# Where the second LayerNorm is done: per batch in attention, or per group after the rows are read back

## The reference

```python
x = x + tanh(g_xattn[0]) * attn(layernorm(x), ctx, ctx, gamma)    # 16 batches, 8 heads, [16, 128, 512] f32
x = x + tanh(g_ffn[0])   * ffn(layernorm(x), ...)                 # 2048 rows of 512
def layernorm(x):                                                 # no scale, no bias
    return (x - mean(x, -1)) / sqrt(var(x, -1) + 1e-5)
def ffn(x):                       # top-2 of 8 experts, hidden 256 to 1024
    h = x @ down_w + down_b
    topv, topi = top_k(softmax(x @ router_w + router_b - 1e-7 * cost), 2)
    gate = softmax(topv)
    out = sum over k, e of gate_k * (topi_k == e) * (gelu(gelu(h) @ w1_e + b1_e) @ w2_e + b2_e)
    out = (out + 0.1 * shared(h)) @ up_w + up_b
    return out + gelu(x) @ core_w + core_b
```

## Time and profile before

| | us |
|---|---|
| median of 3 runs (lowest, highest) | 695.79 (694.21, 697.62) |
| the profiled execution's own time | 693.51 |
| its span, first to last instruction | 690.6 |
| PE busy in the span | 651.6 (94%) |
| DVE | 515.6 (75%) |
| ACT | 531.1 (77%) |
| POOL | 468.1 (68%) |

### The profile page before, as it was taken

One profiled execution on the slowest core, in us unless ns is written; L12 is line 12 of the kernel. 1 busy time (PEld: TensorE's weight loads), 2 busy tenths in 40 slices (PEclk: granted clock), 3 DMA queues, 4 the chain that ended last, 5 costly groups with the idle time before them and its releaser, 6 DMA issues.

```text
span 690.6 us, 18438 instructions
## 1 busy us (share of the span) xinstructions
PE 651.6 (94%) x6005; PEld 342.6 (50%) x6005; DVE 515.6 (75%) x859; ACT 531.1 (77%) x1125; POOL 468.1 (68%) x468
## 2 busy tenths in 40 slices
PE   1799999999999999999999999989999999999998
PEld 0122222222222222222345655579999998998744
DVE  3989999999999999999789877853444434444466
ACT  2389999999999999999888568567777776776411
POOL 3688898888888879986737443506756656665722
PEclk9999999999999999999999999999999999999999
DMA  6755776666767666656335653579988998696596
GB/s 195 249 168 195 221 242 199 194 187 189 221 197 228 198 180 202 190 173 210 113 123 170 228 190 123 171 166 173 125 146 116 127 130 109 99 122 91 61 299 252
DMA packets 128482, 120.40 MB, mean 174 GB/s; under 512 B 64132, under 2 KB 97668, under 8 KB 128392
## 3 DMA queue, kind: packets, MB, share of 16 engines
q1 hardware_dynamic: 114968, 104.09, 53.5%
q0 software_dynamic: 12192, 14.16, 13.7%
q10 hardware_dynamic: 1232, 0.98, 0.5%
HBM read 60.25 MB, written 49.10 MB: 158 GB/s over the span
## 4 chain that ended last, share of the span: by engine, by line
PE 65%; DMA 13%; POOL 11%; DVE 4%; ACT 3%; issue 2%; SPq 2%; POOLq 0%; DVEq 0%
PE EH L1333 23%; PE Y L1333 15%; PE pv L571 11%; PE ring L558 7%; PE nat L546 4%; DMA QS<-q_scratch 2%; DMA q_scratch<-qhl 2%; ACT P L642 2%; POOL wlo L812 1%; DMA u<-in_wall 1%; DMA rd<-den_scratch 1%; DMA QS<-mrow 1%; DMA k_scratch<-khl 1%; POOL y_sums L2235 1%; DMA x_rows<-ao 1%
## 5 line engine op out<-in xcount | busy, mean ns | idle before, releaser
L717 DVE TENSOR_REDUCE mx<-nat 128x2 f32<-128x1024 f32 x256 | 296.6, 1212 | 14.1 <-PE nat L546 13.8
L642 ACT ACTIVATE P<-ring 128x512 f32<-128x512 f32 x512 | 281.1, 601 | 16.8 <-PE ring L558 10.9
L2235 POOL DMA_INDIRECT y_sums<-ysb,to x74 | 124.8, 1687 | 81.6 <-DVE ysb L2165 62.5
L571 PE MATMUL pv<-P,VT 128*32 128x256 f32 x2048 | 157.6, 391 | 0.4
L546 PE MATMUL nat<-KS,QS 48*128 48x512 f16 x512 | 113.1, 394 | 20.2 <-DMA QS<-q_scratch 14.0
L558 PE MATMUL ring<-QS,KS 49*128 49x512 f16 x512 | 119.3, 391 | 9.1 <-ACT P L642 6.8
L1333 PE MATMUL EH<-XA,whi 128*128 128x256 f16 (+1 forms) x688 | 104.9, 258 | 0.5 <-DMA XA<-g_rows 0.5
L1333 PE MATMUL Y<-whi,u 128*128 x592 | 104.3, 273 | 0.2
L571 PEld LDWEIGHTS pv<-P,VT 128*32 128x32 f32 x2048 | 43.9, 108 | 99.1 <-issue 49.1
L2115 DVE TENSOR_TENSOR u<-X,u 128x512 f16<-128x512 f32 x62 | 42.7, 689 | 62.1 <-ACT u L1739 59.0
L558 PEld LDWEIGHTS ring<-QS,KS 49*128 49x128 f16 x512 | 30.7, 93 | 111.1 <-ACT P L642 88.5
(11 more groups left out here) (282 smaller groups left out, 1039.2 us busy)
## 6 DMA issues: line engine op xcount, KB each, us to landing
QS<-q_scratch SPq DMA_DIRECT2D x64, 96.0 KB, 2.7
KS<-k_scratch SPq DMA_DIRECT2D x62, 96.0 KB, 2.3
u<-in_wall SPq DMA_DIRECT2D x7, 640.0 KB, 4.0
X<-in_x SPq DMA_DIRECT2D x16, 256.0 KB, 3.3
q_scratch<-qhl SPq DMA_DIRECT2D x16, 256.0 KB, 2.2
xr<-in_x SPq DMA_DIRECT2D x16, 256.0 KB, 3.5
rd<-den_scratch SPq DMA_DIRECT2D x16, 256.0 KB
u_rows<-un SPq DMA_DIRECT2D x16, 256.0 KB
```

The lines of the kernel that those rows point to most:

```text
L571: m = pe.matmul(pv[32 * j:32 * j + 32, q], VT[i][:, lb, g, j, :], Pb[4 * (s % 2) + j][:, q], start=(lb == 0 and half == 0), stop=(lb == 3) ...
L642: act.activation(Pb[4 * (s % 2) + j][:, :], bank[:, :], ACT.Exp).then_inc(t_use.sem, 1)
L717: dve.tensor_reduce(mx[:, k // 8, :, k % 8], nat[k % 2][:, :, :], AX.X, ALU.max).then_inc(t_max.sem, 1)
L2235: pool.indirect_dma_start(out=ysum[:, :], out_offset=bass.IndirectOffsetOnAxis(ap=to[:, j % 2, a:a + 1], axis=0), in_=ysb[j % 2][:, a, :], ...
```

## The change

Batches 0 to 3 (group 0) are left as they were. For batches 4 to 15 attention does no second LayerNorm: `xstats`, `xaggr`, `xnegm`, `xveps`, `xrstd` and `u` go; SP stores the raw rows `ao` to u_rows as soon as `x1` is done, and `x1t` writes to `un`, which goes to x_rows. So `nb` of a later batch waits for the store to u_rows, where it waited for that to x_rows. Each of the groups 1 to 3 is normalised in its buffer: `row_stats(r)` on DVE, then `normed(r)` on POOL, for which PE's `uT` waits.

```diff
 dve_small(w):
-               ([(w - 3, "xstats"), (w - 3, "xaggr")] if w >= 3 else []) + \
+               ([(w - 3, "xstats"), (w - 3, "xaggr")] if 3 <= w < 3 + G4 else []) + \
 pool_jobs(w):
         if w >= 3:
-            jobs += [(w - 3, n) for n in ("xnegm", "xveps", "xrstd", "u", "x1t")]
+            if w < 3 + G4:
+                jobs += [(w - 3, n) for n in ("xnegm", "xveps", "xrstd", "u")]
+            jobs.append((w - 3, "x1t"))
 sync, window w, s = w - 3:
-                ck.wait(t_pool, s, "u")
-                sp.dma_start(us[s], un[:, :]).then_inc(t_us.sem, 16)
+                ck.wait(t_pool, s, "u" if s < G4 else "x1")
+                sp.dma_start(us[s], un[:, :] if s < G4 else ao[s % 2][:, :]).then_inc(t_us.sem, 16)
 tensor, uT:
-                if i == 0:
-                    wait(pe, t_uu[r % 2], r)
                 for t in range(G4):
+                    if i == 0 and r == 0:
+                        wait(pe, t_uu[0], r)
+                    elif i == 0:
+                        wait(pe, t_nu, r, t)
+        def row_stats(r):
+            wait(dve, t_uu[r % 2], r)
+            for t in range(G4):
+                if r > 1:
+                    wait(dve, t_mv, r - 1, t)
+                dve.bn_stats(sx[:, t, :], ub[r][:, t, :]).then_inc(t_sx.sem, 1)
+            for t in range(G4):
+                wait(dve, t_sx, r, t)
+                if t == 0 and r > 1:
+                    wait(dve, t_ln, r - 1, "veps")
+                dve.bn_aggr(mv[:, t, :], sx[:, t, :]).then_inc(t_mv.sem, 1)
 low_0:
+            row_stats(1)
 rest, after each of DVE's operations o:
-                    if o == (1, "r", "ms"):
-                        ends["late"]["vector"]()
+                    if o == (1, "gl", 1):
+                        row_stats(2)
+                    elif o == (0, "core", G4 - 1):
+                        row_stats(3)
+        def normed(r):
+            wait(pool, t_mv, r, G4 - 1)
+            if r > 1:
+                wait(pool, t_nu, r - 1, G4 - 1)
+            pool.tensor_scalar(ln[:, :, 0], mv[:, :, 0], -1.0, None, ALU.mult).then_inc(t_ln.sem, 1)
+            pool.tensor_scalar(ln[:, :, 1], mv[:, :, 1], EPS, None, ALU.add).then_inc(t_ln.sem, 1)
+            wait(pool, t_ln, r, "veps")
+            pool.tensor_tensor(ln[:, :, 2], ln[:, :, 1], cst[:, K_PH:K_PH + 1].broadcast_to([P, G4]), ALU.pow).then_inc(t_ln.sem, 1)
+            wait(pool, t_ln, r, "rstd")
+            for t in range(G4):
+                pool.tensor_scalar(ub[r][:, t, :], ub[r][:, t, :], ln[:, t, 0:1], ln[:, t, 2:3], ALU.add, ALU.mult).then_inc(t_nu.sem, 1)
 rest, POOL:
+            normed(1)
             for r in BODIES:
                 for o in seq("pool", r):
...
                     elif o == (0, "sc", G4 - 1):
                         last_norm()
+                        normed(2)
+                    elif o == (1, "sc", G4 - 1):
+                        normed(3)
```

More of the change, by code:

```diff
@@ L196, in program @@
             "rbb": sb("rbb", [P, G4, E]), "tb": sb("tb", [P, L]), "lp": sb("lp", [P, L]),
+            "mv": sb("mv", [P, G4, 2]), "ln": sb("ln", [P, G4, 3]),
             "gb": sb("gb", [P, NT]), "zs": sb("zs", [P, LAT]), "Z": sb("Z", [P, LAT]),
@@ L491, in body @@
             if s >= 0:
-                ck.wait(t_pool, s, "u")
-                sp.dma_start(us[s], un[:, :]).then_inc(t_us.sem, 16)
+                ck.wait(t_pool, s, "u" if s < G4 else "x1")
+                sp.dma_start(us[s], un[:, :] if s < G4 else ao[s % 2][:, :]).then_inc(t_us.sem, 16)
                 ck.wait(t_pool, s, "x1t")
-                sp.dma_start(x1s[s], ao[s % 2][:, :]).then_inc(t_st.sem, 16)
+                sp.dma_start(x1s[s], ao[s % 2][:, :] if s < G4 else un[:, :]).then_inc(t_st.sem, 16)
                 tail.get((w, "loads"), lambda: None)()
@@ L515, in last_x1 @@
             sp.wait_ge(t_pool.sem, t_pool.at[B - 1, "x1t"])
-            sp.dma_start(x1s[B - 1], ao[(B - 1) % 2][:, :]).then_inc(t_st.sem, 16)
+            sp.dma_start(x1s[B - 1], un[:, :]).then_inc(t_st.sem, 16)
         def last_u():
-            sp.wait_ge(t_pool.sem, t_pool.at[B - 1, "u"])
-            sp.dma_start(us[B - 1], un[:, :]).then_inc(t_us.sem, 16)
+            sp.wait_ge(t_pool.sem, t_pool.at[B - 1, "x1"])
+            sp.dma_start(us[B - 1], ao[(B - 1) % 2][:, :]).then_inc(t_us.sem, 16)
         late["sync"] = last_x1, last_u
@@ L722, in body @@
                 small(ck, *job)
[L724 to L728, removed]
         over_windows(dve, body, tail)
@@ L741, in job @@
             elif what == "nb":
-                ck.wait(t_st, b - 2)
+                ck.wait(t_st if b - 2 < G4 else t_us, b - 2)
                 done(pool.tensor_scalar(ao[i][:, :], U[1][:, :], cme[:, 1:2], 1.0, ALU.mult, ALU.mult))
@@ L767, in job @@
             elif what == "x1t":
-                ck.wait(t_pool, b, "u")
-                done(pool.tensor_tensor(ao[i][:, :], ao[i][:, :], keep["tb"][:, :], ALU.add))
+                ck.wait(t_pool, b, "u" if b < G4 else "x1")
+                if b == G4:
+                    ck.wait(t_us, b - 1)
+                elif b > G4:
+                    ck.wait(t_st, b - 1)
+                done(pool.tensor_tensor((ao[i] if b < G4 else un)[:, :], ao[i][:, :], keep["tb"][:, :], ALU.add))
             elif what == "negm":
@@ L832, in last_norm @@
         def last_norm():
-            for what in ("xnegm", "xveps", "xrstd", "u", "x1t"):
-                job(Clock(pool), B - 1, what)
+            job(Clock(pool), B - 1, "x1t")
         def last_rows():
@@ L913, in ffn @@
     uf = A("uf", [P, LB, L])
+    mv, ln = keep["mv"], keep["ln"]
     gbs = u[:, :, :].rearrange("p t q -> p (t q)").bitcast(F16)
@@ L933, in ffn @@
     ro, wo, bo, eo = (A(n, [P, NJ], I32) for n in ("ro", "wo", "bo", "eo"))
+    sx = ro[:, 0:6 * G4].bitcast(F32).rearrange("p (t c) -> p t c", t=G4)
     bcur = A("bcur", [P, 2, 8])
@@ L998, in ffn @@
     scattered = lambda r, i: t_sf[i - 2] if r == 0 and i >= 2 else t_sc[i]
+    t_sx, t_mv, t_ln, t_nu = T("f_row_stats"), T("f_row_mean"), T("f_row_scale"), T("f_normed")
     t_zr = T("zero_rows", 16)
@@ L1068, in ffn @@
                 tally.plan(*o)
+    for r in range(1, NG):
+        for t in range(G4):
+            for t_ in (t_sx, t_mv, t_nu):
+                t_.plan(r, t)
+        for what in ("negm", "veps", "rstd"):
+            t_ln.plan(r, what)
     for r in range(NG):
@@ L2075, in set_up, with low_0 @@
             do(0, "lpc", 0)
-        def select_0():
+        def low_0():
             for o in ops_0[LB + 1:upto((0, "r", "dz"))]:
                 do(*o)
-        def low_0():
             dve.wait_ge(t_in2.sem, t_in2.value)
+            row_stats(1)
             for o in ops_0[upto((0, "r", "dz")):upto((0, "gl", 1))]:
@@ L2166, in collect @@
                               ALU.mult).then_inc(t_dve.sem, 1)
-        return {(B - 2, "recip"): set_up, (B - 2, "xstats"): select_0, (B - 1, "recip"): low_0}, rest
+        return {(B - 2, "recip"): set_up, (B - 1, "recip"): low_0}, rest
     def gpsimd(pool):
@@ L2242, in rest @@
                 pool.tensor_tensor(*summands(n), ALU.add).then_inc(t_pool.sem, 1)
-        return {(2, "whi"): output_bias, (B - 3, "xnegm"): some(("uhp", 0), ("uhp", 1)),
+        return {(2, "whi"): output_bias, (B - 3, "x1t"): some(("uhp", 0), ("uhp", 1)),
                 (B - 2, "att"): some(("uhp", 2), ("uhp", 3))}, rest
```

## The result

The changed kernel took 700.36 us (median, 699.37 to 703.54) against 695.60 us of the kernel before in the same comparison: a ratio of 1.0080, 95% interval 1.0064 to 1.0097, 4.8 us between the medians. The prediction was 699.3 (695.0 to 702.7), with 0.48 on no change and 0.45 on slower by over 0.5%. It is slower by 0.8%, with the whole interval above 0.5%: the outcome that had 0.45, not the one that had 0.48. The time came out near the forecast, but partly from other places: two of its terms after attention were far off, in opposite directions.

A forecast was written before the change was run, and what follows sets the result against it. The prediction took PE and ACT, not DVE, to set the pace of attention. Its terms, -0.5 + 0.2 + 1.6 + 2.2 = +3.5 us, on 695.79 gave 699.3 us, with a range of all from 695 to 702.7.

The forecast's parts named there:

- The pace of attention: Attention windows: PE and ACT make the period, DVE follows with some 0.24 us to spare; removing its work gains 0.
- The first rival: Attention: DVE was the pace after all, giving -2.6 us in total, 693.2 us; chance 0.12.
- POOL and the store, -0.5: Attention: nb waits for the earlier u_rows store, so late queries land sooner; -0.5 us (0 to -1).
- Statistics of group 1, +0.2: DVE ahead of gl of group 0: the second gl comes late for PE's rt; +0.2 us (0 to 1).
- Normalising group 1 hidden: POOL after attention: 4.3 us of work ends before ACT copies uT's first tile; 0 (up to 1.5).
- PE found waiting for `uT`: After attention: a sign that would make the prediction wrong; no idle of PE before uT of group 1 was expected.
- Statistics of group 2, +1.6: DVE between second gl and Gp of group 1: PE's gt waits; +1.6 us (0.9 to 2.3).
- Statistics of group 3 hidden, up to 0.5: DVE ahead of gul and ul of group 2: PE reads ul late enough to hide 2.75 us; up to 0.5.
- Normalising group 3, +2.2: POOL ahead of gl of group 2: gl follows 4.3 us later and PE's rt waits; +2.2 us (1.6 to 2.9).
- more waits than counted: Rival, after attention: POOL held up by DVE in all three normed, larger stalls; +6.9 us, 702.7 us; chance 0.2.

The follow-up runs named there:

- e6: Kernel before, with the statistics of windows 7 to 15 taken over 8 of 512 columns, so less DVE time; 695.07 us, 1.0006.
- e9: Changed kernel in which POOL's nb also waits for the x_rows store of two batches before; 701.19 us, 1.0105.
- e5: e1 with row_stats(3) moved on DVE behind ul(1) of group 2; 695.04 us, 1.0018 of the kernel before.
- e10: e5 with row_stats(1) behind gl(1) of group 0 instead of ahead of both gl; 704.13 us, 1.0159 of the kernel before.
- e1: Changed kernel with normed(3) moved behind POOL's first gl of group 2; 696.28 us, 1.0032 of the kernel before.
- e2: Changed kernel with row_stats(3) one operation earlier on DVE, ahead of the last core of group 0; 700.70 us, 1.0090.
- e3: e2 with normed(3) also moved on POOL ahead of group 1's last scatter; 697.27 us, 1.0041 of the kernel before.
- e8: Kernel before with two more bn_stats per window on DVE in windows 7 to 15; 702.93 us, 1.0142.
- e11: Kernel before, unchanged, run again as a control; 695.11 us, 1.0010.
- e12: Changed kernel, unchanged, run again; 701.62 us, 1.0115 of the kernel before.
- e4: e3 with row_stats(1) also moved ahead of DVE's wait for the tables; 697.17 us, 1.0041 of the kernel before.

## Why the prediction was right or wrong

*The pace of attention: right, and shown.* DVE follows with 0.17 us to spare per window (I read 0.24 from the idle). The change took 0.68 us a window from it for nothing. The first rival, DVE as the pace, falls with e6. That the period is made by PE and ACT instead is still argued from the waits of the earlier trace rows: no run changed their work.

*POOL and the store, -0.5: wrong, shown by e9.* I tied the windows that ran over 19.95 us to queries that are late because of `nb`. From window 8 on the longest window is 20.22 us before and 20.04 in the changed kernel's two profiles, but the stretch up to the `uf` copy is no shorter there. It was a guess, and took the only gain of the sum.

*Statistics of group 1, +0.2: mis-sized.* 0.65 us at `rt`, of which 0.18 is given back before `rk` of group 1; 0.47 stays (+0.49 in e5). My time for the second `gl` was good: 364.05 forecast, 363.29 + 0.68 = 363.97 measured. That is partly luck: the statistics began 0.52 us later than I had them (358.46), behind a wait that I had not counted, and a `gat` instruction between the two `gl` that took 1.25 us before took 0.16. And PE came there 0.39 us sooner than before, and I had summed the two as if they were independent: what PE gains ahead of a wait for DVE, the wait takes back.

*Normalising group 1 hidden: right in cost, not to the letter.* PE found waiting for `uT` was to be a sign that the prediction is wrong, and `uT` does wait 0.42 us for its tiles. But the wait for ACT behind it shrinks from 1.55 to 0.71 us, and `a` is then as far behind (+0.28) as `rt` was (+0.26): it costs nothing. e10 shows what it costs 3 us later.

*Statistics of group 2, +1.6: wrong in size, 0.23.* The largest error among the terms that I had worked out. DVE was not 0.4 us later against PE at this place, as I had assumed from group 1, but 0.1 (`msum` 0.18 us later, `rk` 0.08). And the `pk` operations went from 1.35 to 0.29 us and `carry` from 0.50 to 0.17, 1.39 us of holds gone where I counted 0.5. POOL before, then DVE and POOL after:

```profile
383.27 1.26 POOL L769 TENSOR_TENSOR ao<-ao,tb 128x512 f32<-128x512 f32 x1
```

```profile
381.64 2.46 DVE L2072 BATCH_NORM_STATS2 ro<-u 128x6 f32<-128x512 f32 x4
...
384.81 0.29 DVE L1860 TENSOR_TENSOR pk<-rk,m 128x32 f32<-128x32 f32 x2
...
383.17 1.28 POOL L771 TENSOR_TENSOR un<-ao,tb 128x512 f32<-128x512 f32 x1
```

POOL's `x1t`, which had stood beside `pk` (383.34 in the earlier trace rows), now falls on `bn_stats`, and that is not slowed (2.46 us for four here and 2.46 in front of `gul`, where POOL only issues scatters). By the forecast's own sum, with these: 2.75 - 0.25 - 0.8 + 0.1 - 1.39 = 0.41. The Trainium skill's SBUF — State Buffer, section Who interferes with whom, puts the conflict on DVE operations with two SBUF inputs or in a two-port mode; `bn_stats` with one input left alone agrees. I had used that rule for the upper end only, and not asked which DVE instruction would meet POOL's long one after the move.

*Statistics of group 3 hidden, up to 0.5: this step failed, 1.94 us.* I argued from the reader of `ul`, PE, which needs it 3.8 us later. But the statistics stand ahead of `gul`, and the one who waits for `gul` is not its reader: it is ACT, which may not overwrite `uf`. To name what is queued behind, and who reads its result, is not enough: the writers of what the queued instruction reads may wait as well. e5 shows it: same work, six instructions later, 0.01 us.

*Normalising group 3, +2.2: right in mechanism, 2.83 measured, shown by e1.* The slack of 2.18 us held. The term that was mis-sized is the length of `normed`: from 408.04 to 412.90 it is 4.86 us instead of 4.3, mostly since `pow` on four columns takes 1.04 us and not the 0.61 that one column took on average.

*The sum.* -0.5 + 0.2 + 1.6 + 0 + 2.2 = 3.5 was forecast; the table has 5.08 at `rt` of group 3 (5.47 without the offset that attention starts with). Two errors, 1.4 too much and 1.9 too little, nearly cancelled. That 699.3 was within 1.1 us of the median is partly luck. The rival "more waits than counted" (6.9 us) is about as near to the profile's 5.1 as the forecast is (1.8 us off against 1.6), but it gave the place of the 1.94 us only 0.5. The ranges had slips too: the upper bounds of the four terms add up to 0 + 1 + 2.3 + 2.9 = 6.2 us, 702.0 and not 701, and the range of all begins at 695 although the first rival gives 693.2.

The version nearest to the kernel before is e5: 1.0018, with the 0.47 us of group 1 in it. No version beats the kernel before. The change won nothing in attention, so better placing can only bring its price down.

## What to carry to other kernels

Before taking work from the busiest engine, find out whether it waits for the others once in each period; if it does, even 98.7% busy is no bound, and the gain is nothing, while the work can cost time where it is put instead. When work is put ahead of an instruction, ask who reads its result and also who wants to overwrite what it reads. The same 2.75 us cost 1.94 us or nothing, six instructions apart, and an earlier gap is of no use when the data have not landed.

## What the runs showed of the hardware

**A stand of PE (a stretch in which it is idle) can cost more than its length.** The kernels in which PE stands for some 2.65 us before `rt` of group 2 (the changed one twice, e2, e9) show a mean granted clock below 1.0 in 23 of 32 executions. The kernels without it (e1, e3 to e8, e11) show it in 31 of 84. e10, with its stand of 2.85 us before `uT`, shows it in 6 of 6. In the profiles of e2 and e12 the place can be seen, in those of the changed kernel and e9 the clock stays up there. Two stretches behind the wait in e12, columns as above:

```profile
416.00:418.00 2.00, 2.00 (x7) 0.70 (x5) 0.41 (x1) 0.49 (x1) 1.11 (x1) 0.57 0.35 130
418.00:420.00 2.00, 2.00 (x8) 0.95 (x7) 0.00 (x0) 0.00 (x0) 0.96 (x1) 0.57 0.34 127
```

PE stood until 414.99; then the granted clock is 0.57 (0.50 in e2, from 416 to 418 us), that is the lower level, 1.2 GHz, for most of the stretch or all of it, and from `rt` to `gt` it takes 4.71 us instead of 3.03: 1.7 us on top of the 2.83. In the profile of e4 PE waits 3.41 us for a transfer in attention, up to 78.42 us, and from 78 to 84 us the granted clock is 0.50 as well. Such drops would explain why the two comparisons of the changed kernel (1.0080, 1.0115, with overlapping intervals) differ and why its slower executions reach 703.5 and 707.7, but no run sets the length of the stand apart from all else, so that is argued.

**POOL's long operations hold some DVE instructions with one input as well**, though not `bn_stats` above. In e5 a `tensor_scalar` of 128x32 took 1.80 us instead of 0.18 (407.10 in the changed kernel), and ended with POOL's `gl` (406.31 + 1.16). It started 0.6 us ahead of that `gl`, while POOL issued a scatter; why it wasn't done by then is not shown.

```profile
405.71 1.80 DVE L1819 TENSOR_SCALAR pexp<-pexp 128x32 f32<-128x32 f32 x1
...
406.31 1.16 POOL L2217 TENSOR_TENSOR gl<-gf,gh 128x512 f16<-128x512 f32 x1
```

**POOL's `pow` grows with columns:** 0.57 us for most of those with 128x1 (0.61 on average, with one of 1.12), 1.04 to 1.12 for 128x4, but 1.60 in group 1 of e3, e4 and e9.
